# Attention with alibi bias: the keys written into their own tile, projected ahead of the transposes

## What is computed

```
B, S, _ = inputs.shape
qkv = inputs @ W_qkv                   # 32 query heads, 16 key/value heads of 64
k = jnp.repeat(k, NUM_QUERIES, axis=1) # two query heads share a key/value head
scores = einsum('bhqd,bhkd->bhqk', q, k) / sqrt(HEAD_DIM) + slope * (kpos - qpos)
scores = where(causal, scores, -inf)
out = einsum('bhqk,bhkd->bhqd', softmax(scores), v)
return out.transpose(...).reshape(B, S, Q_DIM) @ W_out
```

## Time and profile before

| what | us |
|---|---|
| median of three runs | 3826.7 |
| the profiled execution | 3817.18 |
| its span, first to last instruction | 3815.2 |
| PE busy in the span | 3342.0 (88%) |
| DVE, ACT, POOL busy | 2369.6, 2099.5, 1181.8 |
| mean granted clock of PE | 0.934 of 2.4 GHz |

### The profile page before, as it was taken

One profiled execution on the slowest core, in us unless ns is written; L12 is line 12 of the kernel. 1 busy time (PEld: TensorE's weight loads), 2 busy tenths in 40 slices (PEclk: granted clock), 3 DMA queues, 4 the chain that ended last, 5 costly groups with the idle time before them and its releaser, 6 DMA issues. The chain is left out here.

```text
span 3815.2 us, 72611 instructions
## 1 busy us (share of the span) xinstructions
PE 3342.0 (88%) x22702; PEld 2411.1 (63%) x22702; DVE 2369.6 (62%) x6854; ACT 2099.5 (55%) x4947; POOL 1181.8 (31%) x1820
## 2 busy tenths in 40 slices
PE   5888888888888888888899999797999985799995
PEld 3555555555555555555588888454666655688885
DVE  5666666666666666666666666454666645566665
ACT  4666666566666566666555555322666551355553
POOL 4333233333333333333433433003332300243442
PEclk9999999999999999999999999896999995899998
DMA  2212212221222222112433333211111114355454
GB/s 86 49 39 48 48 43 48 48 48 38 48 48 45 45 48 48 38 43 49 130 122 127 129 130 121 83 39 47 27 31 27 31 25 152 126 138 136 121 139 150
DMA packets 175948, 280.43 MB, mean 74 GB/s; under 512 B 32850, under 2 KB 117586, under 8 KB 175826
## 3 DMA queue, kind: packets, MB, share of 16 engines
q1 hardware_dynamic: 161234, 258.94, 23.8%
q0 software_dynamic: 14592, 19.93, 3.2%
HBM read 159.79 MB, written 41.16 MB: 53 GB/s over the span
## 5 line engine op out<-in xcount | busy, mean ns | idle before, releaser
L771 POOL TENSOR_SCALAR at_p<-at_p,at_recip 128x512 f32<-128x512 f32 (+3 forms) x1030 | 532.0, 533 | 1222.3 <-DVE at_recip L910 1222.3
L820 ACT ACTIVATE at_p<-at_p,at_nmax 128x512 f32<-128x512 f32 (+3 forms) x1032 | 571.5, 554 | 381.6 <-DVE at_nmax L904 378.3
L904 DVE CUSTOM_DVE_ANT_0 at_p<-at_s_ps,at_bias 128x512 f32<-128x512 f32 (+3 forms) x1032 | 462.3, 488 | 54.1 <-PE at_s_ps L1035 45.9
L916 DVE COPY at_pT<-at_t_ps 128x512 f32<-128x512 f32 (+3 forms) x512 | 238.1, 486 | 248.0 <-PE at_t_ps L1047 244.7
L1035 PE MATMUL at_s_ps<-at_k_twice,at_q 64*128 64x512 f32 (+3 forms) x3096 | 382.5, 368 | 4.5 <-DVE at_nmax L904 4.4
L1875 DVE CUSTOM_DVE_ANT_0 aa_a_ps<-aa_a_ps,aa_hidden 128x128 f32<-128x128 f32 (+3 forms) x512 | 247.2, 507 | 173.8 <-PE aa_a_ps L2039 170.7
L827 ACT ACTIVATE at_pT<-at_t_ps 128x512 f32<-128x512 f32 (+3 forms) x512 | 209.2, 434 | 262.5 <-PE at_t_ps L1047 262.5
L1057 PE MATMUL at_o_ps<-at_pT,at_v 128*64 128x512 f32 (+3 forms) x2064 | 330.0, 463 | 0.0
L1775 ACT ACTIVATE aa_pT<-aa_b_ps 128x512 f32<-128x512 f32 (+1 forms) x384 | 196.6, 529 | 175.8 <-PE aa_b_ps L2057 172.9
L1047 PEld LDWEIGHTS at_t_ps<-ident,at_p 64*128 64x128 f32 x5120 | 209.8, 151 | 110.4 <-issue 109.6
L1047 PE MATMUL at_t_ps<-ident,at_p 64*128 64x64 f32 x5120 | 265.3, 245 | 3.4 <-POOL at_p L771 3.2
(11 more groups left out here) (317 smaller groups left out, 8039.6 us busy)
## 6 DMA issues: line engine op xcount, KB each, us to landing
at_k_twice<-at_k_parts SPq DMA_DIRECT2D x260, 256.0 KB, 3.6
w_raw<-in_w_dram SPq DMA_DIRECT2D x57, 768.0 KB, 5.8
nw_w_raw<-in_w_all_dram SPq DMA_DIRECT2D x26, 1024.0 KB, 4.9
nw_w_raw<-in_w_all_dram SPq DMA_DIRECT2D x52, 512.0 KB, 6.8
nw_xh<-xh_dram SPq DMA_DIRECT2D x10, 512.0 KB, 4.1
nw_xl<-xl_dram SPq DMA_DIRECT2D x10, 512.0 KB, 4.7
at_w_raw<-in_w_heads_dram SPq DMA_DIRECT2D x18, 256.0 KB, 4.4
nw_x<-in_x_dram SPq DMA_DIRECT2D x9, 512.0 KB, 5.9
```

Of the source, the lines that this page charges most:

```text
L771: pool.tensor_scalar(p, p, recip[:, u:u + 1], 1.0, ALU.mult, ALU.mult).then_inc(scaled, 1)
L820: act.activation(p_sb[:, u, 0:N], p_sb[:, u, 0:N], ACT.Exp, bias=nmax[:, u:u + 1], scale=-1.0, accum_out=total[:, u:u + 1]).then_inc(exped, 1)
L904: dve.tensor_tensor_reduce(out=p_sb[:, u, 0:N], in0=s_ps[u % 2][:, score_at(u // 2)], in1=bias[:, u % 2, S - N:S], scale=1.0, scalar=BIG, ...
L916: dve.tensor_copy(pT[par][:, :, 0:qt + 1, qt * P:qt * P + HD], turned_half(0)[:, :, turned_at(j), :])\
```

## The change

The tile `k_parts` goes. ACT writes the high part of the keys, and DVE the low part, straight into rows 0 to 63 of `k_twice[par]`; one DMA copies these to rows 64 to 127. `k_copied` then counts 16 per unit. ACT no longer waits for an earlier copy ahead of the high part.

On PE `project_kv(t + 2)` stands right behind `weigh(t - 1)`, ahead of `turn(1)`, `turn(2)` and the scores of blocks 1 and 2. Its last wait (`pair_turnable`) takes over the wait for the scaled and copied blocks, and the one for the copied values. `weigh` waits in its place for the outputs of t-2 to be added. On ACT `take_o` and the keys' high part stand ahead of the turned copies 1 and 2, the values' part behind them, and the queries ahead of the last turned copy and of four exponentials instead of two. On DVE `values`, `rest_o` and `k_rest` stand ahead of the turned copies 1 and 2; `values` first waits for `summed`; the last turned copy stands ahead of `q_rest`.

```diff
             def copy_k(count, par):
                 sp.wait_ge(proj_out, count)
-                for half in range(2):
-                    sp.dma_start(k_twice[par][HD * half:HD * half + HD, :, :].bitcast(F32), k_parts[0:HD, :, :].bitcast(F32))\
-                        .then_inc(k_copied[par], 16)
+                sp.dma_start(k_twice[par][HD:P, :, :].bitcast(F32), k_twice[par][0:HD, :, :].bitcast(F32))\
+                    .then_inc(k_copied[par], 16)
...
-            def take_kv(count, par, half=None):
+            def take_k(count, par):
                 act.wait_ge(proj, count)
-                if half is not None:
-
-                    act.wait_ge(k_copied[1 - par], half * 32 + 32)
-                act.activation(k_parts[0:HD, 0, :], m_ps[par][0:HD, :], ACT.Copy).then_inc(k_high, 1)
+                act.activation(k_twice[par][0:HD, 0, :], m_ps[par][0:HD, :], ACT.Copy).then_inc(k_high, 1)
+
+            def take_v(par):
                 act.activation(vT[HD:P, :], m_ps[par][HD:P, :], ACT.Copy).then_inc(vT_out, 1)
...
                     turn_out(t, 0, par)
                     exps(t + 1, 0)
                     exps(t + 1, 1)
+                    take_o(t, 1 - par)
+                    take_k(kv_count(t + 2), par)
                     turn_out(t, 1, par)
                     turn_out(t, 2, par)
-                    take_o(t, 1 - par)
+                    take_v(par)
                     exps(t + 1, 2)
                     exps(t + 1, 3)
-                    take_kv(kv_count(t + 2), par, pair + par)
-                    exps(t + 1, 4)
-                    exps(t + 1, 5)
                     take_q(q_count(t + 2), par)
                     turn_out(t, 3, par)
-                    exps(t + 1, 6)
-                    exps(t + 1, 7)
+                    for u in range(4, 8):
+                        exps(t + 1, u)
...
                 mask(t + 1, 0)
                 mask(t + 1, 1)
+                dve.wait_ge(summed, t + 1)
+                values(v_count(t + 1), 1 - par)
+                rest_o(t, 1 - par)
+                k_rest(t + 2, par)
                 turn_out(t, 1, par)
                 turn_out(t, 2, par)
-                values(v_count(t + 1), 1 - par)
                 for u in range(2, 6):
                     mask(t + 1, u)
                 invert(t + 1, 0)
-                rest_o(t, 1 - par)
-                k_rest(t + 2, par)
+                turn_out(t, 3, par)
                 q_rest(t + 2, par)
-                turn_out(t, 3, par)
...
+                def pair_turnable():
+                    turnable(t, 1, 3)
+                    pe.wait_ge(proj_out, v_count(t + 1))
...
                 turn(0)
                 score(t + 1, 1 - par, 0, lambda: values_free(t + 1))
                 turn_v(t + 1, 1 - par)
-                weigh(t + (-1), 1 - par, lambda: turnable(t, 1, 3))
+                weigh(t + (-1), 1 - par, lambda: pe.wait_ge(proj_out, out_count(t + (-2), 0)))
+                if new_head is not None:
+
+                    pe.wait_ge(w_split, new_head + 1)
+                project_kv(t + 2, par, b_next, pair_turnable)
                 turn(1)
                 turn(2)
                 score(t + 1, 1 - par, 1)
                 score(t + 1, 1 - par, 2)
-                if new_head is not None:
-
-                    pe.wait_ge(w_split, new_head + 1)
-                project_kv(t + 2, par, b_next, lambda: pe.wait_ge(proj_out, v_count(t + 1)))
                 project_q(t + 2, par, b_next, next_turnable)
```

More of the change, by code:

```diff
@@ L619, in head_attention_phase @@
         k_twice = [sb(f"at_k_twice{i}", [P, 2, S], F32R) for i in range(2)]
-        k_parts = sb("at_k_parts", [P, 2, S], F32R)
         vT = sb("at_vT", [P, S])
@@ L749, in _ @@
                 sp.wait_ge(w_loaded[i], 32 * (KVH // 2 + 1))
-                sp.wait_ge(k_copied[i], 32 * (KVH * B // 2 + 1))
+                sp.wait_ge(k_copied[i], 16 * (KVH * B // 2 + 1))
         @block.gpsimd
@@ L835, in _ @@
             act.sem_inc(odd_out, 1)
-            take_kv(1, 0)
+            take_k(1, 0)
+            take_v(0)
             take_q(2, 0)
-            take_kv(4, 1, 0)
+            take_k(4, 1)
+            take_v(1)
             take_q(5, 1)
@@ L890, in k_rest @@
                 dve.wait_ge(k_high, n + 1)
-                dve.tensor_tensor(k_parts[0:HD, 1, :], m_ps[par][0:HD, :], k_parts[0:HD, 0, :].bitcast(F32),
+                dve.tensor_tensor(k_twice[par][0:HD, 1, :], m_ps[par][0:HD, :], k_twice[par][0:HD, 0, :].bitcast(F32),
                                   ALU.subtract).then_inc(proj_out, 1)
@@ L1068, in next_unit @@
                     turnable(t + 1, 0, 1)
-                    pe.wait_ge(k_copied[par], half * 32 + 64)
+                    pe.wait_ge(k_copied[par], half * 16 + 32)
                 turn(0)
@@ L1101, in _ @@
             project(m_ps[0], 0, 1)
-            pe.wait_ge(k_copied[0], 32)
+            pe.wait_ge(k_copied[0], 16)
             for j in range(TT):
@@ L1105, in _ @@
             pe.wait_ge(proj_out, 5)
-            pe.wait_ge(k_copied[1], 32)
+            pe.wait_ge(k_copied[1], 16)
             pe.wait_ge(even_out, 1)
```

## The result

| | before | after |
|---|---|---|
| median of four runs, us | 3826.1 (3820.4 to 3833.6) | 3460.7 (3459.3 to 3464.5) |
| span of the profiled execution, us | 3815.2 | 3459.7 |
| clock granted in the span | 0.934 | 0.961 |

The ratio is 0.9045 (95% interval 0.9028 to 0.9063). That is 365 us less, where 3560 us had been forecast and 3505 was the lower end of the range: the right direction, and a gain 99 us too small. Ratios are to the kernel before, and are taken over fast executions alone, those at most 1.5% above the fastest of their kernel.

A forecast was written before the change was run, and what follows sets the result against it. It took PE to be bounding the first attention's stage, with query and key waits and clock drops in each body. 128 x (13.93 - 11.84) = 267 us off the median 3826.7 gave 3560 us; range 3505 to 3670, 8 in 10.

The forecast's parts named there:

- Both waits: PE's waits near a body's end, for the queries (0.51 us) and the keys' DMA (1.24): both were to go.
- Full-clock body: 11.44 + 0.30 + 0.10 = 11.84: Loop body of the first attention at full clock: work without the two waits, new wait and reserve, 11.84 us.
- The floor of 11.44: PE's work in one body without the two waits, 13.19 - 1.75 = 11.44 us; if nothing new waits, 3508 us.
- the 1.75 us for the two waits: Cost of PE's query and key waits at the output products, 0.51 + 1.24 us per body.
- The new wait of 0.30: PE before the last block's scores, waiting for DVE's masks: 0.22 us, taken as 0.30 with a restart.
- The reserve of 0.10: 0.1 us per body, 13 us in all, for weight exchanges in 16 bodies and stray waits.
- The clock: Drops of the granted clock in the stage were to go, giving back 0.74 us per mean body.
- The rival in which the drops stay: Same 11.84 body keeps the 0.74 of clock, 12.58: gain 173 us, 3654 us; chance 14%.
- Keys hidden: Single key copy lands 2.9 us after issue, 1.1 us before PE asks; the wait of 1.24 goes.
- Values and queries hidden: DVE's value copy and query rest end before PE asks, with 0.28 and 0.3 us to spare.
- The median: Median of runs lies 9.5 us above the profiled execution; forecast taken off the median, 3560 instead of 3550 us.
- The exponentials: Rival: ACT's exponentials ahead of the keys' high part delay keys by up to 1.3 us: 3726 us; chance 11%.

The follow-up runs named there:

- copy_query_k: copy_query with PE's wait for the keys moved behind the next body's first transposes, right ahead of the scores that read them: 3443.1 us, ratio 0.8976.
- dve_more1: Changed kernel with one extra 128x128 reciprocal on DVE between k_rest and the turned copies, with a wait for its end: 3592.0 us, ratio 0.9379.
- fill_before: Kernel before with four extra 128x512 output products per body, sums overwritten, where PE waits for the keys: 3719.0 us, ratio 0.9712.
- copy_only: Kernel before, order kept, but keys written straight into k_twice and copied by one DMA: 3542.1 us, ratio 0.9247.
- order_only: Changed kernel's order, but keys through their own tile k_parts and two DMAs as before: 3561.5 us, ratio 0.9303.
- proj_late: Changed kernel with PE's key and value projection back behind the scores of blocks 1 and 2: 3615.3 us, ratio 0.9443.
- copy_serial: Changed kernel with the key copy done twice, the second issued when the first has landed, PE waiting for both: 3795.3 us, ratio 0.99.
- dve_more2: Changed kernel with two extra 128x128 reciprocals on DVE between k_rest and the turned copies: 3860.4 us, ratio 1.0043.
- copy_query: copy_only with ACT taking the queries and the last turned copy ahead of exponentials 4 and 5: 3526.4 us, ratio 0.9194.
- kwait_only: Kernel before with only PE's key wait moved behind the next body's first transposes; two copies and old order stay: 3617.3 us, ratio 0.9441.
- query_late: Changed kernel with queries back in their old place: on ACT behind exponentials 4 and 5, on DVE ahead of the last turned copy: 3581.9 us, ratio 0.934.

## Why the prediction was wrong

Both waits and the drops of the clock went, as forecast; the size was off, and one wait that had been added to the sum did not come. The step that failed is "Full-clock body: 11.44 + 0.30 + 0.10 = 11.84", measured 11.16, and with it the lower end of the range, which took 11.44 for a floor.

- *The floor of 11.44 (measured 11.12, 0.32 off, 41 us).* Three of its terms were mis-sized. From a body's first transposes to its value products I took 1.85; it is 1.63 after (1021.57 to 1023.20), and in the median body of before as well. The one body of the earlier trace rows was not typical: it lasts 13.19, and the median of the 29 bodies at full clock is 13.06. For the output products 11.44 leaves 1033.65 - 1030.07 - 1.75 = 1.83; they take 1.64. Against these stands the key projection, 1.60 split off from the queries' where I had 1.49: twelve products in two groups take 0.18 us more than in one (3.19 and 3.01 above), which I had at nothing.

  The output products are where the 1.75 us for the two waits was too small. With both waits the six take 3.72 in the median body of before, and 1.64 after: 2.08. My pitch of 0.25 was too long (0.23 in the rows below), and each wait also slows the products around it. The earlier trace rows had it: 0.34 from 1031.39 to 1031.73 and 0.43 from 1033.22 to the transposes at 1033.65. The same steps where nothing waits, in copy_query_k:

```profile
1018.37 0.40 PE L1007 MATMUL at_m_ps<-at_ol,at_woh 128*128 128x512 f32 x1
1018.60 0.39 PE L1007 MATMUL at_m_ps<-at_oh,at_woh 128*128 128x512 f32 x1
1018.83 0.39 PE L1007 MATMUL at_m_ps<-at_oh,at_wol 128*128 128x512 f32 x1
1019.07 0.40 PE L1007 MATMUL at_m_ps<-at_ol,at_woh 128*128 128x512 f32 x1
1019.39 0.71 PE L1042 MATMUL at_t_ps<-ident,at_p 64*128 64x64 f32 x16
```

  0.23 and 0.32: a restart costs 0.11 each time.
- *The new wait of 0.30 (measured 0, 38 us).* I placed each DVE step behind the full duration of the one before. In the trace after the turned copies start 0.60 behind the start of a k_rest of 0.68 (1016.72 to 1017.32). The trace before shows the same distance, 0.61 behind the q_rest of 0.69 at 1030.64:

```profile
1031.25 0.55 DVE L916 COPY at_pT<-at_t_ps 128x384 f32<-128x384 f32 x1
```

  The four masks are through in 1.11 (1017.85 to 1018.96), not 1.27. Counted from the first key projection product at 1014.39, the turned copies end at 3.53 instead of 3.70 and the masks at 4.57 instead of 4.97. The other part is PE's own: split, it comes to the third query pair at 3.89 instead of 3.72, and to the last scores at 4.84 instead of 4.75. So the turned copies end 0.36 early where I had a tie, and the masks 0.27 early where I had 0.22 late. dve_more1 found 0.28 of cover by its own way. The chain is nearly as tight as was said; it lies on the other side of zero.
- *The reserve of 0.10 (measured 0.04, 8 us).* The bodies with a change of weights take 11.2 instead of 11.12. PE's weight loads wait for the split weights 2.7 us in all.
- *The clock (0.74 given back in full, right).* fill_before prices it at 0.76. The rival in which the drops stay gave 3654, and didn't come. Beside it stood the Trainium skill ("TensorE: Matmul & The Clock Gate", section "A second HAM failure mode: psum-queue depth-cycling"), by which frequent micro-idles between groups of products make the clock swing. The measurement decides against it for waits of this size in this kernel: by their rows copy_only and order_only keep 0.33 and 0.48 us of idle time in each body and proj_late 1.08, and the clock stays at 1.00.
- *Keys hidden (right).* Landing 2.8 after the issue, 2.9 taken; 1.0 us to spare, 1.1 said. Values and queries hidden too. The queries have next to no slack where I had 0.3: q_rest ends at 1020.62, and PE's fourth output product starts at 1020.73, in its turn, but its weight load has waited for them in most bodies:

```profile
PEld at_m_ps L1011 <- DVE at_q L882: 24.1, 113, 0.2
```

- *The median.* The 9.5 us by which the runs of before lie above their profile were carried over to the forecast. After the change the profiled execution (3461.7) and the median agree, and the runs spread by 5 us instead of 13. With 1 us outside the loop and 1 us by which the profile now lies above the median, that makes up the remaining 12.
- *The rivals.* The exponentials never gated: ACT's high part of the keys waits for PE (0.99 us idle), not the other way. That the copy alone or the order alone does most was not among the rivals, and should have been: it was the most useful thing to know.

## What to carry to other kernels

Before a long wait is attacked with a new order of work, move the wait itself to right ahead of the first instruction that reads the data: here one line is worth 212 us, and with one copy and early queries it beats the whole reordering. A wait on PE costs its idle time, a restart (0.11 us here), and, where it is long enough, the clock of what follows (0.76 us a body in before); filling it with useless work is a cheap way to price the clock. To place steps on DVE or ACT, take the distance from start to start in a row of undisturbed ones, not the durations, or every chain comes out longer than it is.

## What was not expected of the hardware

- Extra work made the kernel faster: four more matrix products in each body, 3830 to 3719 us.
- The clock fell in or behind idle stretches at a body's end in before (60 times, with waits of 0.42 and 1.26 us there) and in copy_serial (38 times, one wait of 1.82), and in dve_more2 at another place (81 times, one wait of 1.76). It hardly fell with smaller ones: once each in copy_only (0.33) and copy_query (0.44), 4 times in kwait_only (0.42 and 0.43), never in fill_before (0.42 and 0.35), order_only (0.48), query_late (0.56), dve_more1 (0.74) and proj_late (1.08). What size or spacing of waits is enough isn't settled by these.
- A reciprocal of 128x128 took 0.93 us on DVE, longer than k_rest on 64x512 (0.68).
- Twelve projection products in a row take 3.01 us, in two groups of six 3.19.
